# The second layer's post-attention, routing, experts and store as one block of interleaved half batches

## The reference, cut to what matters

```python
fused = sig * dense_output + (1.0 - sig) * sparse_output
x = _layernorm(src + fused, ln1_g, ln1_b)
ff = jax.nn.relu(x @ ff1_w.T + ff1_b) @ ff2_w.T + ff2_b
return _layernorm(x + ff, ln2_g, ln2_b)
```

## Time and profile before

| | us |
|---|---|
| three runs: median (lowest, highest) | 1875.88 (1872.52, 1876.0) |
| profiled execution, its span | 1874.1 |
| TensorE, VectorE, ScalarE, GpSimd busy | 1327.1, 1205.2, 890.4, 340.9 |
| mean granted TensorE clock | 0.859 |

### The profile page before, as it was taken

How to read it: one execution, slowest core, us unless ns; L and a number is a source line. 1 busy time by engine, 2 the same in 40 slices (tenths; PEclk the granted TensorE clock), 3 DMA queues, 4 the chain that set the end, 5 groups by cost and what they waited for, 6 DMA issues and landing times. The chain is left out here.

```text
span 1874.1 us, 27775 instructions
## 1 busy us (share of the span) xinstructions
PE 1327.1 (71%) x8391; PEld 777.8 (42%) x8392; DVE 1205.2 (64%) x3130; ACT 890.4 (48%) x1180; POOL 340.9 (18%) x368
## 2 busy tenths in 40 slices
PE   4577742899905650899999999999999487246830
PEld 3355532899903420233333333333333355235830
DVE  2655563466666660688888878888888477642442
ACT  2333310334403430888888878888888133012200
POOL 0000012763340003000000000000000023217664
PEclk9888965899957785999999999999999788557975
DMA  6700000343311232222222112121220110202322
GB/s 190 219 0 0 0 12 18 104 115 90 90 34 62 83 107 36 31 36 37 34 35 31 31 32 32 32 31 33 31 32 4 40 53 1 90 13 90 104 70 74
DMA packets 118806, 101.01 MB, mean 54 GB/s; under 512 B 10466, under 2 KB 96192, under 8 KB 118656
## 3 DMA queue, kind: packets, MB, share of 16 engines
q1 hardware_dynamic: 107264, 81.42, 18.9%
q0 software_dynamic: 8192, 16.79, 3.2%
q10 hardware_dynamic: 3248, 1.56, 0.3%
HBM read 56.35 MB, written 43.38 MB: 53 GB/s over the span
## 5 line engine op out<-in xcount | busy, mean ns | idle before, releaser
L1911 ACT ACTIVATE probs<-scores_ps 128x1024 f32<-128x1024 f32 x512 | 508.4, 1026 | 147.5 <-PE scores_ps L1931 144.4
L1931 PE MATMUL scores_ps<-q_pack,k_pack 128*128 128x512 bf16 x1024 | 293.3, 383 | 75.2 <-DMA q_pack<-shift_pieces_dram 48.8
L1948 PE MATMUL pv_ps<-probs,v_pad 128*32 128x512 f32 x2048 | 272.8, 605 | 1.1 <-ACT probs L1911 1.1
L2099 DVE TENSOR_SCALAR_CACHE_REDUCE junk<-sparse_scores,at 128x1024 f32<-128x1024 f32 x192 | 245.6, 1279 | 6.9
L1931 PEld LDWEIGHTS scores_ps<-q_pack,k_pack 128*128 128x128 bf16 x1024 | 72.8, 97 | 363.5 <-ACT probs L1911 168.1
L941 POOL DMA_INDIRECT picked_experts<-expert_rows_dram,pick x128 | 132.9, 1039 | 112.9 <-SPq L1041 44.3
L603 POOL DMA_INDIRECT expert_rows_dram<-expert_input,send x128 | 123.2, 962 | 146.8 <-issue 86.6
L1863 POOL COPY v_pad<-v 128x256 f32 x16 | 6.2, 400 | 639.5 <-PE pv_ps L1948 639.3
L1105 ACT ACTIVATE hidden_experts<-pre_experts 128x512 f32<-128x512 f32 x94 | 59.3, 631 | 107.0 <-DVE pre_experts L1064 66.4
L1127 PE MATMUL up_ps_experts<-x_t_experts,up_weights_now_experts 128*128 128x128 f32 x752 | 104.0, 283 | 0.8 <-ACT x_t_experts L1098 0.7
L1064 DVE TENSOR_TENSOR pre_experts<-up_ps_experts,weights_t 128x512 f32<-128x512 f32 x94 | 64.6, 687 | 57.0 <-PE up_ps_experts L1127 56.9
(11 more groups left out here) (329 smaller groups left out, 2302.2 us busy)
## 6 DMA issues: line engine op xcount, KB each, us to landing
q_pack<-q_pieces_dram SPq DMA_DIRECT2D x144, 64.0 KB
k_pack<-k_pieces_dram SPq DMA_DIRECT2D x144, 64.0 KB
expert_rows_dram<-zeros SPq DMA_DIRECT2D x1, 6400.0 KB, 21.3
x_rows_experts<-expert_rows_dram SPq DMA_DIRECT2D x25, 256.0 KB
expert_rows_dram<-y_rows_experts SPq DMA_DIRECT2D x46, 128.0 KB
expert_rows_dram<-zeros SPq DMA_DIRECT2D x1, 3584.0 KB, 31.2
x_rows_experts<-expert_rows_dram SPq DMA_DIRECT2D x5, 640.0 KB, 4.6
q_pieces_dram<-q_pieces SPq DMA_DIRECT2D x12, 256.0 KB, 2.4
```

The source lines that it names most:

```text
L1911: act.activation(probs[:, kt % 2, j, :], scores_ps[n % 2][:], ACT.Exp, scale=SCALE1).then_inc(exp_done, 1)
L1931: ins = pe.matmul(scores_ps[n % 2][:, c * 512 : c * 512 + 512], k_pack[:, group % 2, j, kt * P : kt * P + P], q_pack[:, group % 2, j, c * ...
L1948: ins = pe.matmul(pv_ps[32 * j : 32 * j + 32, c, :], v_pad[:, group % 2, kt, j, :], probs[:, kt % 2, j, c * 512 : c * 512 + 512], start=(k ...
L2099: step(dve.tensor_scalar(junk[:], s[:, t, :], at[:, t : t + 1], None, ALU.is_ge, ALU.add, accum_out=count[:, t : t + 1]))
```

## The change

`finish_attention`, the second `route`, `experts1` and `store` go; one block, `tail`, comes in their place, without loops. Each engine's program is written out by one function, `in_stages`, to which it gives its share of every step. The unit is half a batch, four tiles; there are eight. Expert work of a batch is cut into 11 steps (k = 0 turns the rows, 1 to 9 go up for expert k-1 and down for expert k-2, 10 turns back and has the rows stored and gathered). The 22 steps of batches 0 and 1 are spread over the rounds 5 to 9, those of batches 2 and 3 follow the rounds:

```diff
+    steps = [(b, k) for b in range(B) for k in range(PIECE_STEPS)]
+    early = 2 * PIECE_STEPS
+    first = 5
+    per = [0] * (HALVES + 2)
+    for n in range(early):
+        per[first + n * (HALVES + 2 - first) // early] += 1
...
+    def experts(i, place):
+        for _ in range(per[i] * (place + 1) // 6 - per[i] * place // 6):
+            expert(*steps.pop(0))
...
+    for i in range(HALVES + 2):
+        now, then, oldest = i, i - 1, i - 2
+        if now < HALVES:
+            turn_ctx(now)
+        if oldest >= 0:
+            turn_n3(oldest)
+        experts(i, 0)
+        if oldest >= 0:
+            logits(oldest)
+        if now < HALVES:
+            dense(now)
+        experts(i, 1)
+        if oldest >= 0 and oldest % 2 == 1:
+            best(oldest // 2)
+        if now < HALVES:
+            norm1(now)
+        if 0 <= then < HALVES:
+            turn_n1(then)
+        experts(i, 2)
+        if oldest >= 0 and oldest % 2 == 1:
+            places(oldest // 2)
+        if 0 <= then < HALVES:
+            ff_up(then)
+        experts(i, 3)
+        if 0 <= then < HALVES:
+            ff_down(then)
+        experts(i, 4)
+        if 0 <= then < HALVES:
+            norm2(then)
+            norm3(then)
+        experts(i, 5)
+    gates()
+    combine(0)
+    while steps and steps[0][0] < B - 1:
+        expert(*steps.pop(0))
+    combine(1)
+    while steps:
+        expert(*steps.pop(0))
+    combine(2)
+    combine(3)
...
+def tail(nc, g, f_v, scratch, expert_rows, dram, out_dram):
```

```diff
+    def variance(which, rows):
+        for n in range(HT):
+            step(dve.bn_stats(stats[:, which, n, :], rows[:, n, :]))
+        step.settle()
+        for n in range(HT):
+            ins = dve.bn_aggr(mean_var[:, which, n, :], stats[:, which, n, :])
+        ins.then_inc(var_ready[which], 1)
+    def invert(which, u):
+        mean, var = mean_var[:, which, :, 0], mean_var[:, which, :, 1]
+        dve.wait_ge(root_ready[which], u + 1)
+        step(dve.reciprocal(rough[:, which], root[:, which]))
+        step.settle()
+        step(dve.scalar_tensor_tensor(out=twice[:, which], in0=var, scalar=LN_EPS, in1=rough[:, which], op0=ALU.add, op1=ALU.mult))
+        step.settle()
+        step(dve.scalar_tensor_tensor(out=twice[:, which], in0=twice[:, which], scalar=-0.5, in1=rough[:, which], op0=ALU.mult, op1=ALU.mult))
+        step.settle()
+        step(dve.scalar_tensor_tensor(out=rstd[:, which, u % 2], in0=twice[:, which], scalar=1.5, in1=rough[:, which], op0=ALU.add, op1=ALU.mult))
+        step.settle()
+        dve.scalar_tensor_tensor(out=shift[:, which, u % 2], in0=mean, scalar=-1.0, in1=rstd[:, which, u % 2], op0=ALU.mult, op1=ALU.mult).then_inc(rstd_ready[which], 1)
...
+    def dense(u):
+        dve.wait_ge(hs_loaded[u % 2], 16 * (u // 2 + 1))
+        dve.wait_ge(out_made, outs.number("dense", u))
+        if u >= 2:
+            dve.wait_ge(n_ready[0], u - 1)
+        dve.tensor_tensor(flat(t[:, u % 2]), out_ps[outs.at("dense", u)][:], flat(hs[:, u % 2]), ALU.add).then_inc(out_free, 1)
+        dve.wait_ge(out_free, outs.number("dense", u))
+        variance(0, t[:, u % 2])
+    def norm1(u):
+        invert(0, u)
...
+    def ff_down(u):
+        dve.wait_ge(out_made, outs.number("ff", u))
+        step.settle()
+        dve.tensor_tensor(flat(o[:, u % 2]), out_ps[outs.at("ff", u)][:], flat(yb[:, u % 2]), ALU.add).then_inc(out_free, 1)
+        dve.wait_ge(out_free, outs.number("ff", u))
+        variance(1, o[:, u % 2])
+    def norm2(u):
+        invert(1, u)
+        x = g.x[:, half(u), :]
+        dve.wait_ge(n_ready[1], u + 1)
+        step(dve.tensor_tensor(o[:, u % 2], o[:, u % 2], bc(gain[:, u // 2, :], HT), ALU.mult))
+        step.settle()
+        step(dve.tensor_tensor(x, x, o[:, u % 2], ALU.add))
+        step.settle()
+        variance(2, x)
+    def norm3(u):
+        invert(2, u)
...
+    def combine(b):
+        for h in range(2):
+            dve.wait_ge(picked_here[b][h], 16 * 2 * HT)
+            for k in range(2):
+                for n in range(h * HT, h * HT + HT):
+                    x = g.x[:, b * NT + n, :]
+                    ins = dve.scalar_tensor_tensor(out=x, in0=picked[:, b % 3, k, n, :], scalar=gate[:, b, k, n : n + 1], in1=x, op0=ALU.mult, op1=ALU.add)
...
```

ScalarE's and TensorE's:

```diff
+    def square_root(which, u):
+        act.wait_ge(var_ready[which], u + 1)
+        act.activation(root[:, which], mean_var[:, which, :, 1], ACT.Sqrt, bias=eps[:, 0:1]).then_inc(root_ready[which], 1)
+    def normal(which, u, out, of):
+        act.wait_ge(rstd_ready[which], u + 1)
+        for n in range(HT):
+            ins = act.activation(out[:, n, :], of[:, n, :], ACT.Identity, scale=rstd[:, which, u % 2, n : n + 1], bias=shift[:, which, u % 2, n : n + 1])
+        ins.then_inc(n_ready[which], 1)
...
+    def dense(u):
+        square_root(0, u)
+        if u + 2 < HALVES:
+            act.wait_ge(out_free, outs.number("dense", u))
+            load(u + 2)
+    def norm1(u):
+        if u >= 2:
+            act.wait_ge(turn_made, turns.number("n1", u - 2))
+        normal(0, u, n1[:, u % 2], t[:, u % 2])
...
+        for k in range(FC):
+            slot = ups.at("ff", u, k)
+            act.wait_ge(up_made, ups.number("ff", u, k))
+            act.activation(ff[:, k, :], up_ps[slot][:], ACT.Relu, bias=g.bias(B_FF1 + k)).then_inc(up_free[slot], 1)
+    def ff_down(u):
+        square_root(1, u)
...
```

```diff
+    def dense(u):
+        turned("ctx", u)
+        slot = outs.at("dense", u)
+        after(pe, out_free, outs.number("dense", u) - 2)
+        for i in range(HT):
+            ins = pe.matmul(out_ps[slot][:, i * C : i * C + C], ctx_t[:, u % 2, i * P : i * P + P], g.weights(W_OUT1), start=True, stop=True)
+        ins.then_inc(out_made, 1)
+    def ff_up(u):
+        turned("n1", u)
+        for k in range(FC):
+            slot = ups.at("ff", u, k)
+            after(pe, up_free[slot], ups.emptied_before("ff", u, k))
+            pe.matmul(up_ps[slot][:], g.weights(W_FF1 + k), y_t[:, u % 2, :], start=True, stop=True).then_inc(up_made, 1)
...
```

GpSimd's and SyncE's:

```diff
+    def places(b):
+        pool.wait_ge(send_ready, b + 1)
+        pool.wait_ge(n_ready[2], 2 * b + 2)
+        for k in range(2):
+            for n in range(NT):
+                pool.indirect_dma_start(
+                    expert_rows.rows, bass.IndirectOffsetOnAxis(ap=send[:, b, k, n : n + 1], axis=0), n3[:, b % 3, n, :], None
+                ).then_inc(rows_sent[b], 16)
...
+    def expert(b, k):
+        if k == E + 2:
+            pool.wait_ge(pick_ready, b + 1)
+            pool.wait_ge(y_stored[b], 16)
+            if b >= 3:
+                pool.wait_ge(combined, 2 * (b - 3) + 2)
+            for h in range(2):
+                for k in range(2):
+                    for n in range(h * HT, h * HT + HT):
+                        pool.indirect_dma_start(
+                            picked[:, b % 3, k, n, :], None, expert_rows.rows[0 : B * SLOTS, :], bass.IndirectOffsetOnAxis(ap=pick[:, b, k, n : n + 1], axis=0)
+                        ).then_inc(picked_here[b][h], 16)
...
```

```diff
+    def load(b):
+        sp.wait_ge(rows_sent[b], 16 * 2 * NT)
+        if b >= 2:
+            sp.wait_ge(y_stored[b - 2], 16)
+        sp.dma_start(expert_io[:, b % 2], rows(expert_rows.rows[b * SLOTS : (b + 1) * SLOTS, :])).then_inc(x_loaded[b], 16)
...
+    def expert(b, k):
+        if k == 4 and b + 1 < B:
+            load(b + 1)
...
```

```diff
+step(dve.tensor_scalar(cosig[:], sig[:], -1.0, 1.0, ALU.mult, ALU.add))
+step.settle()
+for of, by in (
+    (g.weights(W_OUT1), sig),
+    (g.row("L1_attn_out_proj_b"), sig),
+    (g.weights(W_V1), cosig),
+    (g.row("L1_attn_Vp_b"), cosig),
+):
+    step(dve.tensor_scalar(of, of, by[:, 0:1], None, ALU.mult))
...
```

```diff
+def with_bias(b):
+    pool.wait_ge(h_ready, b + 1)
+    after(pool, h_stored, 16 * b)
+    pool.tensor_tensor(src[:], h[:], bc(g.row("L1_attn_out_proj_b"), NT), ALU.add).then_inc(src_ready, 1)
...
```

```diff
+        sp.dma_start(
+            hb[:, half], scratch.h[one, 2 * group : 2 * group + 2].rearrange("b n p c -> p (b n) c")
+        ).then_inc(hb_loaded[half], 16)
...
+    rows = g.x[:, bass.ds(b * NT, NT), :]
+    pool.tensor_tensor(rows, rows, gated[:, bass.ds(b, 1), :].to_broadcast([P, NT, C]), ALU.add)
...
-    dve.tensor_scalar(so[:, t, :], misc[:, 0:C], w_sum[:, group % 2, t : t + 1], None, ALU.mult).then_inc(out_ready, 1)
+    dve.wait_ge(hb_loaded[group % 2], 16 * (b * 2 + group // 2 + 1))
+    dve.scalar_tensor_tensor(
+        out=so[:, t, :], in0=misc[:, 0:C], scalar=w_sum[:, group % 2, t : t + 1], in1=hb[:, group % 2, t, :], op0=ALU.mult, op1=ALU.add
+    ).then_inc(out_ready, 1)
     dve.wait_ge(out_ready, b * NT + group * 2 + t + 1)
...
```

```diff
 self.rows = nc.dram_tensor(f"expert_rows{layer}_dram", [self.total, C], F32, kind="Internal").ap()
 clear(self, eng, zeros, sem):
-n = self.total // P
-eng.dma_start(self.rows.rearrange("(p n) c -> p n c", n=n), zeros.unsqueeze(1).to_broadcast([P, n, C])).then_inc(sem, 16)
+n = self.cleared // P
```

(84 more changed lines are left out.)

744 lines of the change are left out of this document (433 added, 311 removed).

## The result

The kernel after takes 1894.45 us (median of four runs, 1893.34 to 1895.14), the kernel before, with one run more than above, 1874.39 (1872.52 to 1876.0). The ratio is 1.0103, 95% interval 1.0089 to 1.0117: slower by 1.0%, where 0.6% was forecast (1887 us). The profiled execution took 1893.34 us, its span is 1891.3.

The account below looks back on a forecast made before the run. It took a chain of waits across engines as the bound, halves not overlapping. Block 297.6 + 99 = 397 against 389.6, +7, elsewhere +4: 1885 us profiled, forecast 1887 us, slower by 0.6%; range 1848 to 1925, own range 1875 to 1905.

Parts of the forecast that it names:

- The rounds: New block: ten rounds of half a batch, 32.5 us each without additions, last send block starting 297.6 us after the block's start.
- the halves stand in one queue: Rounds: each step needs the one before across three engines, so halves do not overlap; 32.5 us per half, chance 0.42.
- 3.6 + 1.9: ff_up in a round: 3.6 us for half the columns, 1.9 more for first instructions at 1.2 GHz after idling.
- The expert steps: Rounds 5 to 9: 22 steps of 2.18 us on TensorE, showing 0.7 to 1.7 by place; ff_up gets 2 back.
- Wholly hidden: Rival for rounds 5 to 9: expert steps cost nothing there (-12 us), total 1875 us, no change; chance 0.13.
- Behind the last sends: From the last send block to the end: 99 us, 101 less than the 200 of before, including a wait for batch 1's gather.
- the upper end of +7: ScalarE's roots: if every Sqrt cost two table loads, 0.3 us shows 24 times, +7 us; the forecast took 0.
- so I take 2: prepare and attend: GpSimd's new additions slow VectorE's 1024-wide instructions beside them; 2 us taken, between 0 and 13.
- The bound of 13: prepare and attend: at most 8 x 1.6 = 13 us of VectorE delay beside GpSimd's new additions.
- TensorE at 2.4 GHz throughout: Rival for the rounds: TensorE's clock stays high, saving 39 us, 1848 us, or 1867 with half; chance 0.35, time 1862.
- 1.2 GHz throughout: Rival for the rounds: TensorE's clock stays low, 5 us more in each of eight rounds, 1927 us; chance 0.10.
- the wide range: Whole kernel: from the faster clock rival's end, 1848 us, to the slower one's, 1925 us.

Follow-up runs that it names:

- e7: Kernel after with only the order of steps in a round changed, ff_up of the half before directly behind dense; 1839.37 us, ratio 0.9814 to the kernel before.
- e3: Kernel after with TensorE kept busy in rounds 1 to 4 by matmuls whose results nobody reads; 1881.56 us, ratio 1.0032 to the kernel before.
- e2: Kernel after with all 44 expert steps behind the rounds and combine(0) behind the experts of batch 1; 1921.01 us, ratio 1.0239 to the kernel before.
- e4: Kernel after with combine(1) moved behind the experts of batch 3 on all engines; 1887.44 us, ratio 1.0063 to the kernel before.

## Why the prediction was right, point by point

**The rounds**, by the turn of n3, in us from the block's start:

| | forecast | after |
|---|---|---|
| norm 3 of half 0 done | 43.9 | 45.5 |
| half 1 (round 2) | 76.4 | 79.4 |
| half 2 | 112.1 | 114.9 |
| half 3 | 144.6 | 148.3 |
| half 4 | 180.8 | 184.5 |
| half 5 | 214.4 | 217.9 |
| half 6 | 251.4 | 256.0 |
| half 7 | 282.1 | 286.6 |
| last send block | 297.6 | 300.9 |
| end | 397 | 398.9 |

The claim that carried the forecast, that the halves stand in one queue, is shown by e7: the order alone, with the same instructions, takes 55 us out. In the terms the largest miss is ff_up: 3.6 + 1.9 were taken; 6.53 was measured in round 2, of which 2.6 are the clock's (e3), 5.53 and 5.93 in rounds 3 and 4. `best` took 3.2 us from 1579.6 (3.6 forecast), four normalisations 1.65 (1.6), Sqrt 0.30 (0.3), the wait before the logits' turn 10.46 (idle of 11).

**The expert steps.** With the clock that they give back, the nine of rounds 5 and 6 cost nothing (-0.5 and -0.7 us), where the forecast had 0.5 and 1.1; the thirteen of rounds 7 to 9 cost 10.9 (e2). "Wholly hidden" was wrong by 9.5 us, and e2 shows that the steps save 35 for it. The match of rounds 5 and 6 (36.2 and 33.6 forecast, 36.25 and 33.40 measured) is in part luck: without steps they take 36.77 and 34.13 (e2), where the forecast had 35.7 and 32.5, and the steps' price, net, was taken 1.0 and 1.8 too high.

**Behind the last sends** 98.0 us (99 forecast): combine(1) done 44.3 after their start (45.6), gather 3 begun at 68.8 (69.5). The wait for batch 1's gather was seen beforehand and is worth 7 us (e4).

**Table loads.** One at the first Sqrt, one at the Exp, 1.283 us each, none among 24 roots and all Relus; the upper end of +7 did not come. The sentence of the Trainium skill, page ScalarE: Activation LUTs, section Table sets: the hidden batching unit, that relu, copy and identity are in every set, is what this trace shows in the block, where its advice to batch by set would have spoken against Sqrt among Relus. In `prepare` the same trace disagrees: in each of its four batches a load stands at the Copy (L1451) as well as at the Sqrt (L1468). `prepare` is a loop and the block is not; whether that is the reason is not shown.

**Where it failed: "so I take 2" for prepare and attend.** The price of one meeting was right (1.5 us against the 1.6 of the earlier trace rows), the number of meetings was taken as nearly none, "in attend ScalarE and VectorE both have gaps". There were four, each on VectorE's 1024-wide instruction behind its copy out of PSUM: in all four batches GpSimd's addition comes at that moment of the loop, 0.64 or 0.65 us ahead of L1994. TensorE's longer waits make 9.5 of the 6.0 us. The bound of 13 held it. Of the 6 us by which the trace's span missed the forecast's 1885, this is 3.7 (7.7 against 4 ahead of the block) and the block 1.9. `prepare`, for which the same was feared, is not longer. Setup was 2, and attend starts 1.9 earlier than before; that is no larger than what two traces of the same code differ by (707.7 to 710.8).

**The rivals.** TensorE at 2.4 GHz throughout: the clock was 0.63 to 0.70 in rounds without experts, so it fell, but e3 shows its price as worked out, 4.2 a round. Its total of 39 us was too large: for rounds 5 to 7 it counts 3.7 each, though the forecast had already given ff_up its 1.9 back there, which leaves 2.4. 1.2 GHz throughout: ff_down ran at full clock (3.81 us for 32), it fell. The upper end of the wide range, 1925, is 2 us under the 1927 from which it is taken. The forecast's own range, 1875 to 1905, held the result.
